# One written-out order for five engines: convolution attention, cosine linear attention and a top-2 expert layer

## The chip, the cores and the metric

The kernel runs on one core of a Trainium2 chip. Its time is the device time of one execution in microseconds (us); the median of several executions is compared. A core has TensorE (PE, matrix products into eight PSUM banks), VectorE (DVE), ScalarE (ACT), GpSimd (POOL) and SyncE (SP). Each works through its own queue in the order in which the program wrote it, and they wait for each other by semaphores.

## The reference

Eight images of 128 channels and 256 positions go through three layers, each with a residual. All numbers are float32.

```python
# layer 0, attention within an image (xf: 128 channels x 256 positions)
q, k, v = wq @ xf + bq, wk @ xf + bk, wv @ xf
sim = softmax(q.T @ k / 8 + (wkm @ xf + bkm), axis=2)
x = x + gamma * (v @ sim.T)
# layer 1, cosine-weighted linear attention over the 8 images: the cumulative sum
# runs over the images, 8 heads of 16; q_, k_ carry sin and cos of the image's angle
n = layernorm(t)
q, k, v = relu(n @ q_w.T + q_b), relu(n @ k_w.T + k_b), n @ v_w.T + v_b
attn[l] = sum(j <= l: (q_[l] . k_[j]) v[j]) / max(sum(j <= l: q_[l] . k_[j]), 1e-6)
t = t + attn @ out_w.T + out_b
# layer 2, two of eight experts for each of 2048 tokens
n = layernorm(t)
w = softmax over the two largest of n @ router_w
t = t + sum(w[e] * ((silu(n @ w1[e]) * (n @ w3[e])) @ w2[e]))
```

## The kernel before

**Front.** Each image i passes some thirty steps on four engines. On TensorE they are `conv_proj_qk`, `conv_proj_v`, `conv_scores`, `conv_turn` (transposes of the probabilities), `conv_out`, then `lin_turn`, `lin_proj_qk`, `lin_proj_v`, `lin_scores`, `lin_scores_turn`, `lin_out_turn`, `lin_out`, then `route_turn`, `route_logits`, `route_rank`. ScalarE evicts PSUM and makes exponentials and, in `route_lean` (L544 to L551), two hyperbolic tangents that give the routing weights. VectorE makes maxima, statistics (`lin_stats`, `lin_moments`), products of q and k with all earlier images (`lin_products`), values, and the routing from `route_top` to `route_slots`. A token's normalisation (`lin_norm` L865, `route_norm` L948) is a VectorE call that subtracts the mean and multiplies by the inverse root. The inverse root is one GpSimd power, `rstd_lin` (L428) and `rstd_ffn` (L435), of a variance to which VectorE has added epsilon (`lin_eps`, `route_eps`).

**Routing to rows.** `route_rank` counts, with products by a triangle of ones, how many tokens before this one chose the same expert; `route_slots` makes of it the row in a buffer `rows_x` in HBM in which each expert has a list of its own. `scatter` (L441), four indirect DMAs for an image on GpSimd's queue, writes the normalised tokens with their weight and destination there.

**Order of the front.** On every engine a loop over steps calls a list of stages, each with a lag: stage s of image i runs in step i + lag. So all engines take the images in lockstep, one step for an image, 20 steps in all. Each kind of PSUM result has one fixed bank, shared by two kinds in places, and `bank_free` makes TensorE wait until the bank's last reader is done.

**Between the stages.** After the last image TensorE counts the tokens of each expert, VectorE makes from the counts, in a dozen small calls, a table of 39 blocks of 128 rows, each with its first row and its expert (L1026 to L1042), and TensorE turns it. Eight DMAs pad the lists of the experts (`pad_lists`, L349), four on SyncE and four on ScalarE. The engines read table entries into registers eight at a time (`table_reader`, L357); the code of SyncE reads the first eight, then waits for the pads and the scatters.

**Expert stage.** For block s SyncE loads 128 rows (ring of 12), TensorE transposes them (`turn_x`), ScalarE evicts the transposed rows, VectorE copies the expert's weights out of a table in SBUF (`weights`), TensorE makes gate and up products (`gate_up`), ScalarE the silu, VectorE the product (`hidden`), TensorE the down product (`down`), VectorE multiplies by the routing weight (`weigh`, L1062), and GpSimd scatters the rows to `rows_y` (L461). The rings are XBT 4, GATE 3, HID 4, WBS 3. Ahead of the first block TensorE runs 16 warm-up matmuls that nobody reads (L778). At the end the two results of each token are loaded in six parts, added to the residual and stored.

Of the kernel before, what the change touches and what calls it, by code (L numbers as in the profile page):

```python
# [7 lines left out]
ALU = mybir.AluOpType  # L8
# [7 lines left out]
P = 128  # L16
B = 8
# [35 lines left out]

# [14 lines left out]
T_ROW, T_EXPERT = range(2)  # L68

# [22 lines left out]
def hybrid_block(nc, x_ch, x_tok, w_conv, w_lin, w_router, w13, w2, vecs, bias_rows, cst_f, cst_tri, cst_dest,  # L92
                 out):
    ctx = ExitStack()
    with ctx:
# [34 lines left out]
        warm = sb("warm", [PROJ + 1, 1])  # L130
# [14 lines left out]
        ve1 = sb("ve1", [P, 2, T])  # L145
        rs1 = sb("rs1", [P, 2, T])
# [17 lines left out]
        ve2 = sb("ve2", [P, 2, T])  # L164
        rs2 = sb("rs2", [P, 2, T])
# [11 lines left out]
        cnt = sb("cnt", [P, E])  # L177
# [23 lines left out]
        y1 = sb("y1", [P, NT, P])  # L201
        y2 = sb("y2", [P, NT, P])
# [16 lines left out]
        ps_aT = bank(BANK_AT)[:, 0:N]
        ps_y = bank(BANK_Y)[:, 0:T * P].rearrange("p (t c) -> p t c", t=T)  # L220

        ps_x2T = bank(BANK_X2T)[:, 0:N]
        ps_log = bank(BANK_LOG)[:, 0:T * E].rearrange("p (t e) -> p t e", t=T)
        ps_rank = bank(BANK_RANK)[:, 0:T * E].rearrange("p (t e) -> p t e", t=T)
        ps_cnt = bank(7)[:, N + 2 * T * E:N + 2 * T * E + E]

        ps_table = bank(7)[0:2, N + 2 * T * E + E:N + 2 * T * E + E + BLOCKS]
        ps_xbT = [bank(n)[:, 0:P] for n in BANKS_XBT]
        ps_yb = [bank(n)[:, 0:P] for n in BANKS_YB]
        ps_warm = bank(5)[:, 0:2 * P]  # L230
        ps_gu = [bank(n) for n in BANKS_GU]
# [3 lines left out]
        ld_x = [sem(f"ld_x{i}") for i in range(B)]  # L235
        ld_vec = sem("ld_vec")
# [26 lines left out]
        ve1_done = sem("ve1_done")  # L263
# [18 lines left out]
        ve2_done = sem("ve2_done")  # L282
# [11 lines left out]
        scattered = sem("scattered")  # L294
# [27 lines left out]
        wb_done = sem("wb_done")  # L322
        yb_done_pe = sem("yb_done_pe")
# [19 lines left out]
        def run_step(step, *stages):  # L343

            for stage, lag, *which in stages:
                if 0 <= step - lag < B:
                    stage(step - lag, *which)
# [22 lines left out]
        def _(sp):  # L370
# [26 lines left out]
            for s in range(BLOCKS):  # L397
# [5 lines left out]
                if s + 1 < BLOCKS:  # L403
                    row = first_row(s + 1)
# [730 lines left out]
```

## Time and profile before

| | |
|---|---|
| median of 3 runs (lowest, highest) | 201.02 us (199.63, 201.24) |
| profiled execution: its time, its span | 201.14 us, 199.3 us |
| TensorE, VectorE, ScalarE, GpSimd busy in the span | 147.9, 126.2, 73.5, 88.2 us |
| mean granted clock of TensorE | 0.858 of full speed |

The span goes from the first to the last instruction that the profiler recorded. A busy share is a mean over stages that are limited by different things, so it is read by stretches. The granted clock has two levels, 2.4 GHz (1.00) and 1.2 GHz (0.50).

### The profile page before, as it was taken

How to read it: one execution, taken by the hardware profiler on the slowest of the kernel's cores; microseconds unless marked ns; L12 is line 12 of the kernel's file. 1: busy time of each engine (PE TensorE's matmuls, PEld its weight loads, DVE VectorE, ACT ScalarE, POOL GpSimd, SP SyncE). 2: the span in 40 equal slices, each digit the busy share in tenths (PEclk: the TensorE clock that was granted, in tenths of full speed). 3: DMA queues.
4: the chain of work that ended last, by engine and by line, in shares of the span. 5: the costliest groups of instructions: out<-in, count | busy, mean ns of one | idle time of the engine just before them, and what ended most of it. 6: DMA issues, size and time to landing. Idle time of an engine off the chain costs nothing.

```text
span 199.3 us, 4128 instructions
## 1 busy us (share of the span) xinstructions
PE 147.9 (74%) x1125; PEld 129.2 (65%) x1125; DVE 126.2 (63%) x464; ACT 73.5 (37%) x222; POOL 88.2 (44%) x94
## 2 busy tenths in 40 slices
PE   0879999999979589684943057999999999992000
PEld 0557788798767457383823045999999999991000
DVE  2526776799989595997365500667767676752263
ACT  2357686667362204221114001444444444440000
POOL 0001111022023718087787750278787878776000
PEclk9999999999999967996555555999999999999555
DMA  5889600000000101011111714223243333110595
GB/s 131 228 265 363 247 3 0 0 3 0 0 5 13 40 0 56 1 43 42 40 57 53 153 48 105 62 79 92 76 100 84 92 92 85 47 53 0 178 251 204
DMA packets 15476, 16.91 MB, mean 85 GB/s; under 512 B 3083, under 2 KB 14032, under 8 KB 15198
## 3 DMA queue, kind: packets, MB, share of 16 engines
q1 hardware_dynamic: 12606, 12.14, 20.8%
q0 software_dynamic: 2272, 4.24, 6.8%
q10 hardware_dynamic: 576, 0.27, 0.8%
q8 instruction: 10, 0.16, 0.4%
q14 instruction: 12, 0.10, 0.2%
HBM read 10.76 MB, written 6.33 MB: 86 GB/s over the span
## 4 chain that ended last, share of the span: by engine, by line
PE 54%; issue 11%; DVE 11%; DMA 8%; POOL 7%; SPq 3%; ACT 3%; POOLq 0%; DVEq 0%; ACTq 0%
PE ps L759 18%; PE ps L768 8%; POOL rows_x L449 4%; PE ps L610 3%; DMA y<-rows_y 3%; PE ps L630 3%; PE ps L750 2%; PE ps L669 2%; PE ps L690 2%; PE ps L595 2%; DVE num L920 2%; DMA XT<-in_x_tok 2%; PE ps L596 2%; PE ps L620 2%; DVE xrow L952 2%
## 5 line engine op out<-in xcount | busy, mean ns | idle before, releaser
L461 POOL DMA_INDIRECT rows_y<-yb,xb x39 | 43.9, 1124 | 21.9 <-DVE yb L1068 21.0
L759 PE MATMUL ps<-xbT,WB 128*128 128x128 f32 x312 | 42.7, 282 | 0.0
L449 POOL DMA_INDIRECT rows_x<-xrow,slot x32 | 32.3, 1008 | 22.8 <-DVE slot L1013 14.2
L759 PEld LDWEIGHTS ps<-xbT,WB 128*128 128x128 f32 x312 | 39.4, 198 | 0.1
L433 POOL TENSOR_TENSOR rs<-ve,CF 128x2 f32<-128x2 f32 x8 | 5.6, 702 | 42.9 <-DVE ve L863 42.9
L1068 DVE TENSOR_SCALAR yb<-ps,xb 128x128 f32<-128x128 f32 x39 | 13.7, 351 | 17.2 <-PE ps L768 17.2
L572 ACT ACTIVATE gate<-ps 128x256 f32<-128x256 f32 x39 | 14.9, 383 | 25.6 <-PE ps L759 25.6
L768 PE MATMUL ps<-W,hid 128*128 x156 | 23.7, 276 | 0.5 <-DVE hid L1051 0.5
L1051 DVE TENSOR_TENSOR hid<-gate,ps 128x256 f32<-128x256 f32 x39 | 16.0, 411 | 11.0 <-ACT gate L572 11.0
L768 PEld LDWEIGHTS ps<-W,hid 128*128 128x128 f32 x156 | 20.5, 192 | 0.7 <-issue 0.7
L566 ACT ACTIVATE xbT<-ps 128x128 f32<-128x128 f32 x39 | 10.8, 277 | 19.3 <-PE ps L750 19.3
L1058 DVE COPY WB<-W 128x512 f32 x39 | 16.3, 421 | 1.5 <-issue 1.5
L750 PE MATMUL ps<-CF,xb 128*128 128x128 f32 x39 | 11.2, 287 | 1.2 <-DMA xb<-rows_x 1.2
L881 DVE TENSOR_TENSOR qk<-kT,qT 128x1024 f32<-128x1024 f32 (+3 forms) x12 | 11.4, 950 | 0.9 <-ACT kT L517 0.9
L920 DVE TENSOR_TENSOR num<-vt,sco 128x1024 f32<-128x1024 f32 (+3 forms) x12 | 11.4, 953 | 0.1
L690 PE MATMUL ps<-CF,num 128*128 128x128 f32 x72 | 11.1, 308 | 0.0
L714 PE MATMUL ps<-WR,x2T 128*128 128x8 f32 x32 | 5.9, 292 | 5.6 <-DVE where L1004 5.6
L714 PEld LDWEIGHTS ps<-WR,x2T 128*128 128x128 f32 x32 | 5.8, 251 | 6.4 <-issue 6.4
L595 PE MATMUL ps<-X,WC 128*65 128x256 f32 x16 | 5.5, 426 | 5.8 <-DMA XT<-in_x_tok 5.8
L690 PEld LDWEIGHTS ps<-CF,num 128*128 128x128 f32 x72 | 9.4, 160 | 0.0
L610 PE MATMUL ps<-ck,cq 65*128 65x256 f32 x32 | 8.7, 396 | 0.1
L630 PE MATMUL ps<-cv,probT 128*128 128x128 f32 x64 | 8.7, 279 | 0.0
(126 smaller groups left out, 281.2 us busy)
## 6 DMA issues: line engine op xcount, KB each, us to landing
xb<-rows_x SPq DMA_DIRECT2D x39, 65.0 KB, 2.0
W<-in_w SPq DMA_DIRECT2D x1, 2048.0 KB, 10.3
y<-rows_y SPq DMA_DIRECT2D x8, 192.0 KB, 4.8
X<-in_x_ch SPq DMA_DIRECT2D x8, 128.0 KB, 2.9
XT<-in_x_tok SPq DMA_DIRECT2D x8, 128.0 KB, 3.4
W<-in_w SPq DMA_DIRECT2D x1, 1024.0 KB, 12.4
out_tok<-y SPq DMA_DIRECT2D x4, 192.0 KB, 3.6
rows_y<-yb,xb POOLq DMA_INDIRECT x39, 2.4
```

Source lines behind the costliest of these rows:

```text
L449: pool.indirect_dma_start(rows_x, bass.IndirectOffsetOnAxis(ap=slot[:, g:g + 1], axis=0), xrow[:, i * T + t, c, :], None, bounds_check=DUM ...
L461: pool.indirect_dma_start(rows_y, bass.IndirectOffsetOnAxis(ap=xb[:, n, DEST_COL:ROW].bitcast(I32), axis=0), yb[:, n, :], None, bounds_che ...
L572: act.activation(gate[:, s % GATE, :], ps_gu[s % 3][:, 0:F], ACT.Silu).then_inc(gate_done, 1)
L610: last = pe.matmul(ps_sim[:, t, :], cq[:, b, t * P:(t + 1) * P], ck[:, b, :], start=True, stop=True)
L630: last = pe.matmul(ps_co[:, t, :], probT[:, b, k, t * P:(t + 1) * P], cv[:, b, k, :], start=(k == 0), stop=(k == T - 1))
L690: last = pe.matmul(ps_aT[:, t * P:(t + 1) * P], num[:, i % 2, j, t * P:(t + 1) * P], ident, start=(j == 0 and t == 0), stop=(j == i), is_t ...
L750: pe.transpose(ps_xbT[s % 2], xb[:, s % RING, 0:P], ident).then_inc(xbT_done, 1)
L759: last = pe.matmul(ps_gu[s % 3][:, k * P:(k + 1) * P], WB[:, s % WBS, k * P:(k + 1) * P], xbT[:, s % XBT, :], start=True, stop=True)
L768: last = pe.matmul(ps_yb[s % 2], hid[:, s % HID, k * P:(k + 1) * P], W2[:, bass.ds(e * (FK * P) + k * P, P)], start=(k == 0), stop=(k == F ...
L920: dv.tensor_tensor(num[:, b, first:end, :].rearrange("p j (g d) -> p (j g) d", d=D), vt[:, first:end, :].rearrange("p j (g d) -> p (j g) d ...
L1051: dv.tensor_tensor(hid[:, s % HID, :], gate[:, s % GATE, :], ps_gu[s % 3][:, F:2 * F], ALU.mult)\
L1058: dv.tensor_copy(WB[:, s % WBS, :], W13[:, bass.ds(experts[s] * (2 * F), 2 * F)]).then_inc(wb_done, 1)
```

## The change

1. All five queues are written out call by call instead of in lockstep steps. TensorE, VectorE and ScalarE take the calls of different images in one mixed order, and PSUM banks are given call by call (`BANK_CQK = (1, 3, 5, 0, ...)`): any result may stand in any of the eight banks, in one rotation with the others.
2. Both normalisations become ScalarE activations (scale and bias from SBUF columns). The epsilon, a negated mean and the product of it with the inverse root move to GpSimd, two of them with a wait on GpSimd's own results. The weighting of the expert results moves to ScalarE as well.
3. Scatters are written out one by one on GpSimd, with inverse roots of later images among them.
4. Loads: the weights of the first layer, constants, triangles, destinations and router weights go out on ScalarE's queue; the two layouts of an image have a semaphore each, and TensorE waits for the channel layout alone.
5. The table code can make several tables; there is one, of 39 blocks. It stands ahead of the last `route_slots` on VectorE. All eight pads are issued by SyncE, which reads its first table entries after the waits.
6. The table load for the silu (`silu_set`) stands on ScalarE after the last exponential, ahead of six of the eight `route_lean` calls. The warm-up matmuls are gone.
7. Rings: XBT 6, GATE 4, HID 5, WBS 5. In the expert stage TensorE transposes the rows of six blocks in a batch. The arrays of the final sums reuse the inputs' SBUF.

```diff
-XBT, GATE, HID, WBS = 4, 3, 4, 3
-BANKS_XBT, BANKS_GU, BANKS_YB = (0, 1), (3, 4, 6), (2, 5)
+XBT, GATE, HID, WBS = 6, 4, 5, 5
+TABLES = ((8, 39, 0),)
...
-            sp.wait_ge(table_done, 1)
-            first_row = table_reader(sp, T_ROW, DUMMY)
-            row = first_row(0)
-            sp.wait_ge(pads_stored, 16 * (E + 1))
-            sp.wait_ge(scattered, 16 * NT * TOP_K)
...
+                sp.wait_ge(table_done, k + 1)
...
+                    sp.wait_ge(scattered[n], 16 * images * T * TOP_K)
...
+                    sp.wait_ge(pads_stored, 16 * (E + 1))
+                for s in range(first, first + blocks):
+                    load_rows(s)
...
             def rstd_ffn(i):
-                pool.wait_ge(ve2_done, i + 1)
+
+                b = i % 2
+                pool.wait_ge(mv2_done, 2 * (i + 1))
                 if i >= 2:
                     pool.wait_ge(xrow_done, 2 * (i - 1))
-                pool.tensor_tensor(rs2[:, i % 2, :], ve2[:, i % 2, :], CF[:, C_HALF:C_HALF + T], ALU.pow).then_inc(rs2_done, 1)
...
+                pool.tensor_scalar(nm2[:, b, :], mv2[:, b, :, 0], -1.0, None, ALU.mult)
+                link(pool.tensor_scalar(ve2[:, b, :], mv2[:, b, :, 1], LN_EPS, None, ALU.add))
+                link(pool.tensor_tensor(rs2[:, b, :], ve2[:, b, :], CF[:, C_HALF:C_HALF + T], ALU.pow))
+                pool.tensor_tensor(nb2[:, b, :], nm2[:, b, :], rs2[:, b, :], ALU.mult).then_inc(rs2_done, 1)
...
-            for step in range(STEPS):
-                run_step(step, (scatter, 9, 0), (scatter, 9, 1), (rstd_lin, 2), (rstd_ffn, 6))
...
+            rstd_lin(0); rstd_lin(1); rstd_lin(2); rstd_lin(3); rstd_ffn(0); rstd_lin(4); rstd_ffn(1)
+            scatter(0, 0); scatter(0, 1); scatter(0, 2); scatter(0, 3); rstd_lin(5); rstd_ffn(2); scatter(1, 0)
+            scatter(1, 1); scatter(1, 2); rstd_lin(6); scatter(1, 3); rstd_ffn(3); scatter(2, 0); scatter(2, 1)
+            scatter(2, 2); rstd_lin(7); scatter(2, 3); rstd_ffn(4); scatter(3, 0); scatter(3, 1); scatter(3, 2)
+            scatter(3, 3); rstd_ffn(5); scatter(4, 0); scatter(4, 1); scatter(4, 2); scatter(4, 3); rstd_ffn(6)
+            scatter(5, 0); scatter(5, 1); scatter(5, 2); scatter(5, 3); rstd_ffn(7); scatter(6, 0)
...
+            def route_norm(i):
+                b = i % 2
+                act.wait_ge(rs2_done, i + 1)
+                for t in range(T):
+                    act.activation(xrow[:, i * T + t, :, 0:P], t2[:, i * T + t, :].unsqueeze(1).broadcast_to([P, TOP_K, P]),
+                                   ACT.Identity, bias=nb2[:, b, t:t + 1], scale=rs2[:, b, t:t + 1]).then_inc(xrow_done, 1)
...
+            lin_v(3); conv_qk(7); conv_pT(6); conv_v(6); route_lean(1); lin_sums(4); lin_norm(5); conv_exp(7)
+            silu_set(); route_norm(2); lin_xT(5); lin_aT(3); lin_v(4); route_xT(2); conv_pT(7); lin_qk(5)
...
-            for step in range(STEPS):
-                run_step(step, (lin_scores_turn, 5), (lin_proj_qk, 4), (lin_proj_v, 5), (route_rank, 9), (conv_proj_v, 1), (lin_out_turn, 6),
-                         (conv_turn, 2), (conv_scores, 1), (route_logits, 8), (lin_out, 6), (lin_turn, 3), (conv_out, 2),
-                         (lin_scores, 4, 0), (conv_proj_qk, 0), (lin_scores, 4, 1), (route_turn, 7))
...
+            conv_proj_v(0); conv_proj_qk(0); conv_scores(0); conv_proj_qk(1); conv_proj_v(1); conv_proj_qk(2)
+            conv_turn(0); conv_scores(1); conv_proj_qk(3); conv_out(0); conv_scores(2); conv_turn(1)
+            conv_proj_v(2); conv_scores(3); conv_out(1); conv_proj_qk(4); conv_turn(2); conv_proj_v(3)
+            conv_turn(3); lin_turn(0); conv_proj_qk(5); conv_out(2); lin_proj_qk(0); lin_turn(1); lin_proj_v(0)
...
+            conv_proj_v(5); route_turn(0); lin_out(1); lin_out_turn(2); route_logits(0); lin_turn(4)
+            lin_scores(3, 0); conv_out(5); conv_scores(6); route_rank(0); lin_proj_qk(4); lin_out(2)
...
-            for _ in range(WARM_MATMULS):
-                pe.matmul(ps_warm, TRI[:, 0:P], TRI[:, :], start=True, stop=True)
...
+            down(16); gate_up(18); down(17); gate_up(19); turn_x(20); down(18); turn_x(21); turn_x(22)
+            turn_x(23); turn_x(24); turn_x(25); gate_up(20); down(19); gate_up(21); gate_up(22); down(20)
...
+            route_where(6); route_slots(6); route_top(7); route_index(7); route_gap(7); route_mask(7)
+            route_seen(7); route_weights(7); route_where(7); table_rows(0); route_slots(7); table_copy(0)
```

## Rows read from the trace of the kernel before

**Rows 1.** The page's busy tenths, 40 slices of 5 us.

```profile
PE   0879999999979589684943057999999999992000
DVE  2526776799989595997365500667767676752263
ACT  2357686667362204221114001444444444440000
POOL 0001111022023718087787750278787878776000
```

**Rows 2.** Windows: us, busy (instructions) of PE, PEld, DVE, ACT, POOL; clock, DMA, GB/s.

```profile
70.00:71.00 1.00, 0.28 (x3) 0.30 (x3) 1.00 (x3) 0.00 (x0) 0.00 (x0) 0.96 0.00 0
77.00:78.00 1.00, 1.00 (x5) 0.82 (x5) 0.76 (x4) 0.00 (x0) 0.73 (x1) 0.63 0.28 83
125.00:126.00 1.00, 1.00 (x9) 1.00 (x8) 0.71 (x2) 0.00 (x0) 0.00 (x0) 0.74 0.37 75
130.00:150.00 20.00, 20.00 (x182) 20.00 (x181) 13.98 (x42) 9.19 (x28) 15.73 (x15) 1.00 0.33 86
```

**Rows 3.** The chain that ended last: start, us, what; the last scatter.

```profile
116.98 2.28 DMA rows_x<-xrow,slot
```

**Rows 4.** Timeline of GpSimd, 60 to 120 us: start, us, what, [idle before].

```profile
62.78 1.19 POOL L449 DMA_INDIRECT rows_x<-xrow,slot  x1 [4.46 <-DVE slot L1013]
...
107.91 0.97 POOL L449 DMA_INDIRECT rows_x<-xrow,slot  x1 [0.30 <-issue]
109.18 0.97 POOL L449 DMA_INDIRECT rows_x<-xrow,slot  x1 [0.30 <-issue]
```

**Rows 5.** Timeline of all engines, from the count to the last block.

```profile
108.90 0.17 DVE L1026 COPY cnt<-ps 128x8 f32<-128x8 f32 x1 [0.35 <-PE ps L742]
...
109.98 1.93 SPq L355 DMA_DIRECT2D rows_x<-pad  x4
...
111.36 0.14 DVE L1042 TENSOR_SCALAR steer<-exp_f 39x1 f32<-39x1 f32 x1
...
113.45 1.12 DVE L1058 COPY WB<-W 128x512 f32 x3 [1.45 <-issue]
...
121.49 1.01 PE L750 MATMUL ps<-CF,xb 128*128 128x128 f32 x2 [1.18 <-DMA xb<-rows_x]
...
180.48 0.71 PE L768 MATMUL ps<-W,hid 128*128 x4 [0.52 <-DVE hid L1051]
```

**Rows 6.** The same chain at 21 us: TensorE at full clock.

```profile
21.51 0.45 PE ps L602 x4
...
22.39 0.87 PE ps L610 x4
```

**Rows 7.** Waits: who waited for whom: us in total, times, longest.

```profile
PE ps L595 <- DMA XT<-in_x_tok: 5.8, 1, 5.8
```

**Rows 8.** DMA issues: count, size, median us to landing.

```profile
xb<-rows_x SPq DMA_DIRECT2D x39, 65.0 KB, 2.0
...
X<-in_x_ch SPq DMA_DIRECT2D x8, 128.0 KB, 2.9
...
WC<-in_w_conv SPq DMA_DIRECT2D x1, 129.0 KB, 2.5
```

**Rows 9.** Groups by line: count, busy us, mean ns of one, idle before.

```profile
L439 POOL TENSOR_TENSOR rs<-ve,CF 128x2 f32<-128x2 f32 x8 | 5.9, 743 | 0.0
L425 POOL COPY xrow<-DEST 128x32 int32<-128x32 int32 x1 | 0.2, 240 | 7.3 <-DMA DEST<-in_cst_dest 7.3
L423 POOL MEMSET pad<- 128x1 int32 x1 | 0.1, 102 | 0.0
L488 ACT ACTIVATE cv<-ps,VEC 128x256 f32<-128x256 f32 x8 | 3.8, 473 | 1.1 <-PE ps L602 1.1
L536 ACT ACTIVATE attT<-ps 128x256 f32<-128x256 f32 x8 | 3.1, 384 | 7.7 <-PE ps L690 7.7
L566 ACT ACTIVATE xbT<-ps 128x128 f32<-128x128 f32 x39 | 10.8, 277 | 19.3 <-PE ps L750 19.3
L558 ACT ACT_TABLE_LOAD x1 | 1.3, 1283 | 0.0
```

More of the change, by code:

```diff
@@ L68 @@
 T_ROW, T_EXPERT = range(2)
+NO_EXPERT = 1 << 14
 def constants():
@@ L293, in hybrid_block @@
         slot_done = sem("slot_done")
-        scattered = sem("scattered")
+        scattered = [sem(f"scattered{k}") for k in range(len(TABLES))]
         cnt_done = sem("cnt_done")
@@ L322, in hybrid_block @@
         wb_done = sem("wb_done")
+        wb_loaded = [sem(f"wb_loaded{n}") for n in range(WBS)]
         yb_done_pe = sem("yb_done_pe")
@@ L341, in pieces, with table_of @@
             return sum(len(halves(i)) for i in range(n))
[L343 to L347, printed above, removed]
-        def pad_lists(eng, experts):
-            eng.wait_ge(pad_row_done, 1)
-            held = [eng.alloc_register(f"pad_row{e}") for e in experts]
-            eng.reg_load(held, pad_row[0:1, experts[0]:experts[-1] + 1])
-            for reg in held:
-                row = eng.snap(reg, min_val=0, max_val=DUMMY - P)
-                eng.dma_start(rows_x[bass.ds(row, P), :], pad[:, :]).then_inc(pads_stored, 16)
+        def table_of(s):
+            return [k for k, (_, _, first) in enumerate(TABLES) if first <= s][-1]
         def table_reader(eng, line, most):
             sets = [[eng.alloc_register(f"line{line}_{half}_{n}") for n in range(READ)] for half in range(2)]
+            turn = [1]
             def read(s):
-                held = sets[s // READ % 2]
-                if s % READ == 0:
-                    m = min(READ, BLOCKS - s)
-                    eng.reg_load(held[0:m], table[line:line + 1, s:s + m])
-                return eng.snap(held[s % READ], min_val=0, max_val=most)
+                _, blocks, first = TABLES[table_of(s)]
+                n = (s - first) % READ
+                if n == 0:
+                    turn[0] = 1 - turn[0]
+                    m = min(READ, first + blocks - s)
+                    eng.reg_load(sets[turn[0]][0:m], table[line:line + 1, s:s + m])
+                return eng.snap(sets[turn[0]][n], min_val=0, max_val=most)
             return read
@@ L459, in _, with result @@
+            def result(s):
                 n = s % RING
@@ L1070, in _ @@
-            dv.wait_ge(ld_w13, 32)
-            dv.wait_ge(table_done, 1)
-            expert = table_reader(dv, T_EXPERT, E - 1)
-            experts = [expert(0)]
-            for s in range(-3, BLOCKS + 1):
-                if s + 3 < BLOCKS:
-                    weights(s + 3)
-                if s >= 1:
-                    weigh(s - 1)
-                if 0 <= s + 1 < BLOCKS:
-                    hidden(s + 1)
+                dv.tensor_copy(WB[:, s % WBS, :], W13[:, bass.ds(e * (2 * F), 2 * F)]).then_inc(wb_done, 1)
```

665 lines of the change are left out of this document (406 added, 259 removed).

## The prediction, made before the changed kernel ran

> **What bounds the kernel now.** I read the busy tenths first, then the chain that ended last, the timeline around the change of stage, and the groups for prices. The tenths [rows 1] show three stages. Up to the 10th slice (50 us) TensorE fills nearly every slice after the first. From there to the 24th no engine is full for long: TensorE falls from 9 to 0, VectorE stands at 9 and then between 6 and 3, while GpSimd climbs to 7 and 8. From the 26th slice TensorE is full again until the outputs are gathered. So a front with slack is followed by a mixture-of-experts (MoE) stage without any. In the window 130 to 150 us [rows 2] TensorE is busy all 20.0 us with 182 matmuls; a block has 13 (8, 4 and 1 by line), so 14 blocks pass at 1.43 us each. VectorE, ScalarE and GpSimd are busy 14.0, 9.2 and 15.7 us there: no reordering makes that stage shorter than 39 x 1.43 = 55.7 us.
>
> What ends the front is GpSimd. The last row scatter starts at 116.98 us and its data land 2.28 us later [rows 3]. Before it the scatters run back to back: one starts 1.27 us after the other with only "issue" between them [rows 4]. The first of 32 starts at 62.78, having waited 4.46 us for a slot number [rows 4]. So the front is set by when routing of image 0 is ready and by how tightly 32 scatters and the inverse roots, all on GpSimd's queue, follow. The span divides at rows thus: 116.98 to the last scatter; 4.51 to the first row transpose at 121.49 [rows 5]; 59.70 of blocks to the end of the last down projection (180.48 + 0.71 = 181.19 [rows 5]); 18.11 to the end at 199.30.
>
> **First scatter.** The chain gives TensorE's prices at full clock [rows 6]: 0.45 us for four passes of 128 columns (a four-tile transpose is the same), 0.87 for four passes of 256. In TensorE's new order there stand ahead of the first ranking: 7 query/key projections of 0.87 (6.1), 6 value projections (2.7), 7 score pairs (6.1), 6 four-tile transposes (2.7), 6 outputs of eight passes (5.4), and of the linear attention 5 turns, 4 and 3 projections, scores, turns and outputs of up to four images (some 11, priced by the same passes): 34 us. The first matmul waits until 5.80 for the second layout of image 0 [rows 7], which it doesn't read; afterwards it waits for the channel layout and the weights alone, and the weights go out on ScalarE's queue. A channel layout lands 2.9 us after its issue and the weights 2.5 [rows 8], both issued by about 0.8: 3.7 us. With 3 us for the exchanges with ScalarE and VectorE in the first images and 1.8 for ranking to slots, the first scatter starts at 42.5 us instead of 62.78.
>
> **The GpSimd queue after it.** 31 more starts at 1.28 are 39.7 us. Nine inverse-root calls stand among them in the new order (images 5 to 7 of the first normalisation, 2 to 7 of the second). Such a call was one power of 0.743 us [rows 9]; now it is four instructions with two waits on GpSimd's own results. The trace of before has no such small arithmetic on GpSimd. From below, a 128x1 memset takes 0.102; from above, the power itself is a two-operand instruction of 0.743; nearest in kind is a 128x32 copy of 0.240 [rows 9]. I take 0.2 each with one of the three overlapped, and 0.1 for each own wait: 1.4 us, bounds 0.8 and 3.1. Nine are 12.6 us. What waits behind them on the queue: a scatter ready to go, and behind the scatters the roots, so normalisation 6 waits for the scatters of image 4, and 7 for those of image 5. I allow 6 us in which the queue has nothing to do: about 2 for image 2's slots, 1.5 for image 5's moments, 2.5 at the end, because VectorE now makes the block table before the slots of image 7. From the count's copy at 108.90 to the second column at 111.36 that took 2.6 us [rows 5]; in before the slots went first. Last scatter: 42.5 + 39.7 + 12.6 + 6.0 = 100.8 us, 16.2 earlier.
>
> **VectorE and ScalarE.** 32 normalisation calls and the 39 weightings leave VectorE, with 16 additions of epsilon. ScalarE pays more per call: a pointer operand is worth 473 - 384 = 89 ns [rows 9], so weighting costs 0.277 [rows 9] + 0.089 = 0.37, and a normalisation with two pointers 0.46 (128 wide) or 0.56 (256 wide): 16 us in the front. It has the room: 5 to 8 tenths up to the 10th slice, mostly 4 or less after it [rows 1]. In the MoE stage ScalarE goes from 0.66 us a block (9.2 over 14 [rows 2]) to 1.03, under 1.43. I cost it at nothing there: TensorE covers it, and per-block cost would show only above 1.43.
>
> **Between the stages.** SyncE used to read its first registers before it waited for the scatters; now it reads them after. VectorE shows what a read costs: 1.45 us idle with "issue" ahead of its first weight copy [rows 5]. Bounds 0.2 and 1.45; I take 1.3. All eight list pads now go out on SyncE, one after the other, instead of four each on two queues; four took 1.93 to issue [rows 5]. Eight issues at 0.48 end some 4 us after the count and land near the last scatter, which covers them; uncovered they would cost 1 us. Stage: 4.51 + 1.3 = 5.8.
>
> **Blocks.** The 16 warm-up matmuls go. The clock row shows 1.2 GHz up to the middle of 125 to 126 us, some 4.0 us after the first transpose; earlier, with nothing ahead of it, it fell at the end of 70 to 71 and rose again 6.7 us later [rows 2]. At half speed 6.7 us lose 3.35 of work against 2.0: +1.4, bounds 0 and 2. Deeper rings and batches of six transposes move no TensorE work; the sixth transpose of a batch needs a buffer whose result left 7.3 us of TensorE work earlier, and the way round (weighting 0.5, scatter and landing near 2.3 [rows 3], reload 2.0 [rows 8], issue 0.5 each) takes some 6. The end is 0.7 shorter, since the last results queue less. So 59.7 + 1.4 and 18.1 - 0.7.
>
> **Sum.** 100.8 + 5.8 + 61.1 + 17.4 = 185.1 us of span. The profiled execution took 201.14 at a span of 199.3, so 1.84 lie around it: 186.9, say **187 us**. That execution is within 0.1% of the median of 201.02.
>
> **The Trainium skill against the change.** The page "GPSIMD Engine Reference", opening, calls GpSimd the wrong choice for ordinary elementwise arithmetic, VectorE being about twice as fast; this change moves the epsilon and the negated mean there. The trace has only the 0.240 us copy to weigh it with, and neither settles calls on two columns; by twice VectorE's price the call would be about 1.5, and the sum 188. The page "ScalarE: Activation LUTs", section "Table sets: the hidden batching unit", asks to finish one set before going to the next, 2.66 us a switch with the drain. The trace has a load of 1.283 us [rows 9] for the gate's function, after the last hyperbolic tangent; now it stands ahead of twelve of these.
>
> **Rivals.**
> 1. GpSimd nearly packed: the small calls cost their lower bound, image 0 is ready at 40. 40 + 39.7 + 9 x 0.83 + 3 = 90.2, 10.6 less: 176 us. For it: at the end GpSimd's scatters were packed in before too [rows 4]. Against: each image's routing needs a full turn through all engines.
> 2. Slower: each small GpSimd call costs as much as the power. 4 x 0.743 + 0.1 = 3.1 us a call, 1.7 x 9 = 15.3 more on the queue that ends the front: 202 us. It decides from 2.95 us a call (1.4 + 14 / 9). For it: the only two-operand row is 0.743. Against: copy and memset, a third and a seventh of that.
> 3. ScalarE becomes the bound: the hyperbolic tangents have to reload their table (two more loads, one in front of the first gate, 2.6 us), and its written order blocks on inverse roots that wait behind scatters, 2.5 us more: 192 us.
> 4. The order doesn't fill the front: image 0 is ready only at 48, and from first to last scatter it takes as long as before (116.98 - 62.78 = 54.2) plus nine longer calls, 6 us: 108, 7.3 later than my sum: 194 us.
>
> **Chances.** The forecast 0.52, with its own range of 182 to 191; rival 1 0.15, rival 2 0.07, rival 3 0.14, rival 4 0.12. The range 177 to 198 leaves out half of rival 1, rival 2 and the upper end of rival 4, under 0.2; it takes in the bounds of register read and clock, and all of the small calls' but their upper end. A measurement of this kernel tells 1% from nothing (its runs lie 0.8% apart). Faster by over 1%, below 199.0: 0.90; within: 0.04; slower: 0.06.
>
> **What would show it.** Right: the first scatter near 42 and the last near 101 us; TensorE at 8 tenths or more up to some 60 us; inverse-root groups of four instructions at about 1.4 us; blocks again at 1.43; SyncE idle over a microsecond between landing and first load; the low clock for some microseconds more in the first blocks. Wrong: small GpSimd instructions of 0.5 us or more, a third table load, TensorE waiting at every sixth transpose, or scatters that wait for slots for more than 6 us in all.

## The result, and the profile after

The changed kernel takes 204.22 us (median of 4 runs, 203.01 to 205.92), 1.0224 times the kernel before, with a 95% interval of 1.0151 to 1.0298. It is slower, by 1.5 to 3%; forecast was 187.0, 177 to 198. The ratios here and below are estimated from the faster executions alone and are not quotients of the medians, which here give 204.22 / 201.13 = 1.0154. The profiled execution took 203.01 us at a span of 201.1.

The busy tenths of the page, 40 slices of 5.0 us, answer to [rows 1]:

```profile
PE   1899999999959783995453104999999999995000
DVE  2066466969716586479141620354554545531163
ACT  3277997787376643432313001456566565653000
POOL 0002331545868588787777450157667676767000
```

TensorE is full from the 3rd slice to the 10th and VectorE has more room, as forecast. But GpSimd, which climbs earlier, stands at 5 to 8 from the 11th slice to the 22nd: it starts sooner and ends no sooner. The timeline of GpSimd, 40 to 130 us (start, us, what, [idle before]), answers to [rows 4]:

```profile
47.81 2.15 POOL L502 DMA_INDIRECT rows_x<-xrow,slot  x1 [2.12 <-DVE slot L1133]
50.27 0.98 POOL L502 DMA_INDIRECT rows_x<-xrow,slot  x1 [0.31 <-issue]
51.55 2.00 POOL L502 DMA_INDIRECT rows_x<-xrow,slot  x1 [0.30 <-issue]
53.85 0.97 POOL L502 DMA_INDIRECT rows_x<-xrow,slot  x1 [0.30 <-issue]
...
70.61 1.70 POOL L502 DMA_INDIRECT rows_x<-xrow,slot  x1 [1.83 <-DVE slot L1133]
72.61 0.98 POOL L502 DMA_INDIRECT rows_x<-xrow,slot  x1 [0.30 <-issue]
...
80.16 1.81 POOL L489 TENSOR_TENSOR rs<-ve,CF 128x2 f32<-128x2 f32 x1
...
84.32 1.86 POOL L502 DMA_INDIRECT rows_x<-xrow,slot  x1 [0.30 <-issue]
...
87.76 1.64 POOL L502 DMA_INDIRECT rows_x<-xrow,slot  x1 [0.30 <-issue]
89.47 0.23 POOL L487 TENSOR_SCALAR nm<-mv 128x2 f32<-128x2 f32 x1
89.76 0.22 POOL L488 TENSOR_SCALAR ve<-mv 128x2 f32<-128x2 f32 x1
90.06 0.72 POOL L489 TENSOR_TENSOR rs<-ve,CF 128x2 f32<-128x2 f32 x1
90.86 0.20 POOL L490 TENSOR_TENSOR nb<-nm,rs 128x2 f32<-128x2 f32 x1
91.75 1.09 POOL L502 DMA_INDIRECT rows_x<-xrow,slot  x1 [0.70 <-issue]
...
114.26 0.96 POOL L502 DMA_INDIRECT rows_x<-xrow,slot  x1 [2.42 <-DVE slot L1133]
...
118.26 0.97 POOL L502 DMA_INDIRECT rows_x<-xrow,slot  x1 [0.30 <-issue]
```

The first scatter starts 15 us earlier than before and the last 1.3 us later [rows 3, 4]: 31 starts take 70.45 us instead of 54.2. What follows the last scatter is much as forecast. Timelines of SyncE and TensorE, between the stages and at the last block, then the window 130 to 150 (columns as in [rows 2]):

```profile
121.34 4.12 SPq L416 DMA_DIRECT2D xb<-rows_x  x8
...
123.42 0.45 PE L868 MATMUL ps<-CF,xb 128*128 128x128 f32 x1 [9.77 <-DMA xb<-rows_x]
...
183.63 0.71 PE L894 MATMUL ps<-W,hid 128*128 x4 [0.67 <-DVE hid L1193]
...
130.00:150.00 20.00, 20.00 (x182) 20.00 (x181) 10.56 (x28) 12.47 (x42) 13.64 (x14) 1.00 0.29 80
```

Against the sum: first scatter 47.81 (forecast 42.5), from it to the last 70.45 (58.3), to the first row transpose 5.16 (5.8), blocks to 183.63 + 0.71 = 184.34, so 60.92 (61.1), tail 201.1 - 184.34 = 16.76 (17.4). Late by 5.3 and 12.15, early by 1.4: 16.0 us of span. The profiled run lies 1.2 us below the median, which is the rest. Again 182 matmuls pass in 20 us: the bound of the expert stage (TensorE's 1.43 us a block) has not moved.

**Where the 70.45 us are.** Clean scatters: 31 x 1.28 = 39.7. Root calls: the scatter before the call at 89.47 ends at 89.40 and the next starts at 91.75; of these 2.35 us 0.30 would be there anyway, so a call takes 2.05 us of the queue, and nine take 18.5. Waits for slots: 1.83 us at 70.61, of which 0.69 belong to the call ahead, and 2.42 at 114.26, of which 0.30 are usual, so 3.3. Stretched instructions: 9 scatters of 1.05 to 2.15 us instead of 0.97, one at 1.15 and four root instructions lie 9 us above their usual length. Together 70.5. The 54.2 us of before divide as 39.7 + six roots at 0.64 (3.8) + two waits of 4.6 (9.2) + 1.3 of stretch = 54.0, from rows of before that were not shown yet (GpSimd's timeline):

```profile
74.09 1.10 POOL L449 DMA_INDIRECT rows_x<-xrow,slot  x1 [4.88 <-DVE slot L1013]
...
84.65 1.10 POOL L449 DMA_INDIRECT rows_x<-xrow,slot  x1 [4.88 <-DVE slot L1013]
...
101.81 0.74 POOL L439 TENSOR_TENSOR rs<-ve,CF 128x2 f32<-128x2 f32 x1
102.73 1.04 POOL L449 DMA_INDIRECT rows_x<-xrow,slot  x1 [0.18 <-issue]
```

A power alone: the scatter before it ended at 101.79, the next starts at 102.73; 0.94 - 0.30 = 0.64.

**What stretches a scatter.** VectorE's timeline of the changed kernel beside the rows above: `qk` and `num` (L1015, L1052) multiply two operands that both lie in SBUF.

```profile
47.65 1.22 DVE L1015 TENSOR_TENSOR qk<-kT,qT 128x1024 f32<-128x1024 f32 x1
...
51.48 1.23 DVE L1052 TENSOR_TENSOR num<-vt,sco 128x1024 f32<-128x1024 f32 x1
...
73.15 0.95 DVE L1015 TENSOR_TENSOR qk<-kT,qT 128x768 f32<-128x768 f32 x1
...
80.16 1.22 DVE L1052 TENSOR_TENSOR num<-vt,sco 128x1024 f32<-128x1024 f32 x1
...
84.12 1.23 DVE L1015 TENSOR_TENSOR qk<-kT,qT 128x1024 f32<-128x1024 f32 x1 [2.74 <-ACT kT L596]
...
87.35 1.21 DVE L1015 TENSOR_TENSOR qk<-kT,qT 128x1024 f32<-128x1024 f32 x1
```

The scatter at 51.55 meets `num` with 51.48 + 1.23 - 51.55 = 1.16 us to go and takes 2.00; that at 84.32 meets `qk` with 1.03 to go: 1.86; at 87.76 with 0.80 to go: 1.64. Each takes 0.84 plus what the product still has to run, or 0.97 if that is more. In all sixteen traces 63 scatters that follow another scatter begin at least 0.06 us into such a product, and all but one of them keep to this within 0.03 us. A scatter that follows arithmetic or a wait pays up to 0.26 more (the first, with 1.06 to go, takes 2.15). The scatter at 72.61, in whose course a product begins, takes 0.98, and one that begins with the product, within 0.03 us, mostly isn't held either (at 66.01: 1.10). The expert stage gives the other half of the comparison; VectorE and GpSimd of the changed kernel, then of the kernel before:

```profile
145.06 0.41 DVE L1193 TENSOR_TENSOR hid<-gate,ps 128x256 f32<-128x256 f32 x1
...
145.19 0.97 POOL L510 DMA_INDIRECT rows_y<-yb,xb  x1 [0.30 <-issue]
```

```profile
139.68 0.42 DVE L1058 COPY WB<-W 128x512 f32 x1
...
139.80 1.14 POOL L461 DMA_INDIRECT rows_y<-yb,xb  x1 [0.30 <-DVE yb L1068]
```

`hid` has one operand in PSUM: all 11 scatters that start under it, with up to 0.35 us to go, take 0.97. The copy of weights from SBUF to SBUF, with 0.30 to go, gives 1.14 = 0.84 + 0.30, as for the 35 scatters of before that start under it (mean 1.15). So operands decide, not VectorE being busy; e3 and e4 below show it for one product in one place. The Trainium skill has this in "GPSIMD Engine Reference", section "1. Specifications": GpSimd's SBUF interfaces are shared with VectorE, with contention when a VectorE instruction has two SBUF inputs or runs in its two-port mode. The rows of `qk`, `num` and `hid` agree; whether the copy, which has one input, runs in the two-port mode no row shows. The prediction left this out.

### The profile page after: what moved, and what is told of

Read it like the earlier page. It is cut to its first block, busy times and chain, and to the rows that moved or that the text cites. A ratio compares the mean times of both kernels' runs of the same rounds, so it can differ in the third digit from the quotient of the medians.

```text
span 201.1 us, 4097 instructions
## 1 busy us (share of the span) xinstructions
PE 146.7 (73%) x1109; PEld 129.3 (64%) x1109; DVE 101.8 (51%) x377; ACT 97.0 (48%) x294; POOL 102.5 (51%) x142
## 4 chain that ended last, share of the span: by engine, by line
PE 55%; POOL 17%; issue 11%; DMA 7%; DVE 4%; SPq 2%; ACT 2%; POOLq 0%; ACTq 0%; DVEq 0%
PE ps L879 17%; POOL rows_x L502 10%; PE ps L894 8%; PE ps L723 4%; PE ps L804 3%; PE ps L743 3%; PE ps L868 2%; POOL rows_y L510 2%; DMA X<-rows_y 2%; PE ps L707 2%; PE ps L708 2%; PE ps L715 2%; PE ps L759 2%; PE ps L782 2%; DMA WC<-in_w_conv 2%
## 5 line engine op out<-in xcount | busy, mean ns | idle before, releaser
L510 POOL DMA_INDIRECT rows_y<-yb,xb x39 | 37.9, 972 | 28.9 <-ACT yb L661 23.1
L502 POOL DMA_INDIRECT rows_x<-xrow,slot x32 | 38.2, 1194 | 17.6 <-issue 11.3
L1193 DVE TENSOR_TENSOR hid<-gate,ps 128x256 f32<-128x256 f32 x39 | 16.2, 415 | 5.1 <-PE ps L894 3.7
L661 ACT ACTIVATE yb<-ps,xb 128x128 f32<-128x128 f32 x39 | 14.3, 367 | 3.4 <-PE ps L894 1.6
L647 ACT ACTIVATE xbT<-ps 128x128 f32<-128x128 f32 x39 | 8.5, 280 | 13.6 <-PE ps L868 13.6
L868 PE MATMUL ps<-CF,xb 128*128 128x128 f32 x39 | 7.6, 300 | 10.0 <-DMA xb<-rows_x 10.0
L1015 DVE TENSOR_TENSOR qk<-kT,qT 128x1024 f32<-128x1024 f32 (+3 forms) x12 | 11.5, 955 | 5.3 <-ACT kT L596 5.3
L621 ACT ACTIVATE xrow<-t,nb,rs 128x256 f32<-128x256 f32 x16 | 8.7, 593 | 10.1 <-POOL nb L490 10.1
L1052 DVE TENSOR_TENSOR num<-vt,sco 128x1024 f32<-128x1024 f32 (+3 forms) x12 | 11.4, 953 | 1.8 <-ACT vt L609 1.6
L476 POOL TENSOR_SCALAR nm<-mv 128x2 f32<-128x2 f32 x8 | 2.8, 344 | 18.5 <-DVE mv L1007 18.3
L868 PEld LDWEIGHTS ps<-CF,xb 128*128 128x128 f32 x39 | 5.4, 156 | 10.4 <-issue 10.4
L581 ACT ACTIVATE xn<-t,nb,rs 128x128 f32<-128x128 f32 x16 | 7.0, 486 | 8.1 <-POOL nb L479 8.0
L979 DVE TENSOR_REDUCE nmax<-ps 128x2 f32<-128x512 f32 x8 | 5.5, 687 | 10.3 <-PE ps L723 10.2
```

Of the source, the lines that this page charges most:

```text
L502: pool.indirect_dma_start(rows_x, bass.IndirectOffsetOnAxis(ap=slot[:, g:g + 1], axis=0), xrow[:, i * T + t, c, :], None, bounds_check=DUM ...
L510: pool.indirect_dma_start(rows_y, bass.IndirectOffsetOnAxis(ap=xb[:, n, DEST_COL:ROW].bitcast(I32), axis=0), yb[:, n, :], None, bounds_che ...
L661: act.activation(yb[:, n, :], bank(BANK_YB[s])[:, 0:P], ACT.Copy, scale=xb[:, n, W_COL:W_COL + 1]).then_inc(yb_done, 1)
L868: pe.transpose(bank(BANK_XBT[s])[:, 0:P], xb[:, s % RING, 0:P], ident).then_inc(xbT_done, 1)
L1015: dv.tensor_tensor(qk[:, i % 2, first:end, :], kT[:, first:end, :], qT[:, i % 2, :].unsqueeze(1).broadcast_to([P, end - first, N]), ALU.mult)\
L1193: dv.tensor_tensor(hid[:, s % HID, :], gate[:, s % GATE, :], bank(BANK_GU[s])[:, F:2 * F], ALU.mult)\
```

## The experiments

Ratios are to the kernel before, measured on the same chip; the experiments ran on several chips, on which it had medians of 199.99 to 200.72 us, so a difference in us between two of them is good to about 1 us. Theory Q is: GpSimd's queue ends the front, and each microsecond in it counts. Theory O: the order, in which roots stand behind scatters, holds the images.

**e1: small calls off GpSimd.** VectorE adds epsilon and negates, GpSimd makes the power alone, ScalarE the shift `nb`.

```diff
-                pool.tensor_scalar(nm1[:, b, :], mv1[:, b, :, 0], -1.0, None, ALU.mult)
-                link(pool.tensor_scalar(ve1[:, b, :], mv1[:, b, :, 1], LN_EPS, None, ALU.add))
-                link(pool.tensor_tensor(rs1[:, b, :], ve1[:, b, :], CF[:, C_HALF:C_HALF + T], ALU.pow))
-                pool.tensor_tensor(nb1[:, b, :], nm1[:, b, :], rs1[:, b, :], ALU.mult).then_inc(rs1_done, 1)
+                pool.tensor_tensor(rs1[:, b, :], ve1[:, b, :], CF[:, C_HALF:C_HALF + T], ALU.pow).then_inc(rs1_done, 1)
...
```

> The changed kernel, but GpSimd computes only the power: VectorE adds epsilon and negates the mean right after the moments, ScalarE multiplies the negated mean by the root (two 0.2 us calls and an own wait). Theory Q (GpSimd's queue ends the front; a root call of four instructions costs it 2.05 us from the end of one scatter to the next, a single power 0.64): nine calls among the scatters save 9 x 1.4 = 12.7 us, of which some 8 to 12 arrive, 192 to 196 us; last scatter at 106 to 110 us instead of 118. Rival O (the mixed order itself delays the images and GpSimd only waits for them): 203 to 205 us, GpSimd idle longer between scatters.

Measured: 198.69 us, 0.9912 [0.9864, 0.996]; first scatter 49.23, last 114.71. Between the two theories: the last scatter comes 3.5 us earlier, not the 9 x (2.05 - 0.64) = 12.7 that nine calls would give. When a call shrinks, part of it becomes waiting: among its scatters GpSimd now waits some 13 us for moments and slots, against 3.3.

**e2: the kernel before, with three small calls and two own waits beside each power** (their results unread).

```diff
-                pool.tensor_tensor(rs1[:, i % 2, :], ve1[:, i % 2, :], CF[:, C_HALF:C_HALF + T], ALU.pow).then_inc(rs1_done, 1)
+                pool.tensor_scalar(xa[:, 2 * i + 0, :], CF[:, C_HALF:C_HALF + T], -1.0, None, ALU.mult)
+                link(pool.tensor_scalar(xe[:, 2 * i + 0, :], CF[:, C_HALF:C_HALF + T], LN_EPS, None, ALU.add))
+                link(pool.tensor_tensor(rs1[:, i % 2, :], ve1[:, i % 2, :], CF[:, C_HALF:C_HALF + T], ALU.pow))
+                pool.tensor_tensor(xp[:, 2 * i + 0, :], xa[:, 2 * i + 0, :], rs1[:, i % 2, :], ALU.mult).then_inc(rs1_done, 1)
...
```

> The kernel before, in its lockstep order, with three small calls beside each power on GpSimd, as many as in the changed kernel and with the same two own waits, their results unused (nothing is left out). Theory Q: three to six of the calls stand among back-to-back scatters, each 1.4 us longer: 205 to 209 us, last scatter at 121 to 125. Rival O: within 1 us of 201.

Measured: 208.98 us (four runs, 207.02 to 210.75) beside 200.67; the profiled one took 207.78. First scatter 65.56 instead of 62.78, last 124.02 instead of 116.98. GpSimd's timeline:

```profile
107.87 0.22 POOL L454 TENSOR_SCALAR xe<-CF 128x2 f32<-128x2 f32 x1
108.17 0.72 POOL L455 TENSOR_TENSOR rs<-ve,CF 128x2 f32<-128x2 f32 x1
108.97 0.20 POOL L456 TENSOR_TENSOR xp<-xa,rs 128x2 f32<-128x2 f32 x1
109.85 1.09 POOL L466 DMA_INDIRECT rows_x<-xrow,slot  x1 [0.69 <-issue]
```

In the lockstep order too the four instructions cost, some 7 us for sixteen calls: 2.8 ahead of the first scatter and 4.3 behind it, where six of them stand. The next scatter starts 0.69 us after the last of them instead of 0.18. Theory Q holds for the calls' price.

**e3 and e4: one more 128x256 product per block in the expert stage,** on the changed kernel; in e3 both operands in SBUF, in e4 one in PSUM.

```diff
+                link(dv.tensor_tensor(hid[:, s % HID, :], gate[:, s % GATE, :], W13[:, 0:F], ALU.mult))
                 dv.tensor_tensor(hid[:, s % HID, :]
```

> The changed kernel with one extra VectorE product of 128x256 in each of the 39 blocks, both inputs in SBUF (overwritten at once by the right product, after an own wait). Theory C (GpSimd's work stands still while VectorE runs a two-input call with both inputs in SBUF, which stretched scatters of the front from 0.97 to 2.15 us): the block scatters, 0.972 us in the changed kernel, get a longer mean, 1.1 us or more, some of 1.3 to 1.5. Rival T (scatters stretch by their own data or the DMA queue): 0.97 as before. The time within 2 us of 204, VectorE having room.

> The same extra product in the same place with one input in PSUM. Theory C: the block scatters stay at 0.97 to 1.0 us. A theory by which any more VectorE work stretches them: as long as in the SBUF run.

Measured: 208.48 and 207.49 us, one run each, more than the 2 us from 204 that were expected; why stays open. Scatters took 0.995 and 0.986 us on average, because most begin when no extra product runs. The few that begin under one settle it. VectorE and GpSimd of e3, then of e4 (the upper line of each is the extra product):

```profile
184.69 0.42 DVE L1193 TENSOR_TENSOR hid<-gate,W 128x256 f32<-128x256 f32 x1 [0.96 <-PE ps L894]
...
184.81 1.16 POOL L510 DMA_INDIRECT rows_y<-yb,xb  x1 [0.31 <-issue]
```

```profile
183.71 0.42 DVE L1193 TENSOR_TENSOR hid<-gate,ps 128x256 f32<-128x256 f32 x1 [0.96 <-PE ps L894]
...
183.82 0.97 POOL L510 DMA_INDIRECT rows_y<-yb,xb  x1 [0.30 <-issue]
```

Both scatters begin with some 0.31 us of the extra product to go. With both operands in SBUF the scatter takes 0.84 + 0.31, with one in PSUM its usual 0.97. Three more of e3, with 0.18 to 0.19 to go, take 1.02 to 1.04; two more of e4, with 0.15 and 0.19 to go, take 0.97. So theory C's stretch is there and rival T's 0.97 isn't, though with four such scatters of 39 the mean doesn't reach the 1.1 that was expected.

**e5: only GpSimd's order changed,** roots ahead of the scatters of two images earlier.

```diff
-            scatter(0, 0); scatter(0, 1); scatter(0, 2); scatter(0, 3); rstd_lin(5); rstd_ffn(2); scatter(1, 0)
-            scatter(1, 1); scatter(1, 2); rstd_lin(6); scatter(1, 3); rstd_ffn(3); scatter(2, 0); scatter(2, 1)
+            rstd_lin(5); rstd_ffn(2); scatter(0, 0); scatter(0, 1); scatter(0, 2); scatter(0, 3);
+            rstd_lin(6); scatter(1, 0); scatter(1, 1); rstd_ffn(3); scatter(1, 2); scatter(1, 3);
+            rstd_lin(7); scatter(2, 0); scatter(2, 1); rstd_ffn(4); scatter(2, 2); scatter(2, 3);
...
```

> The changed kernel with nothing but GpSimd's written order altered: each inverse root stands one to four calls earlier, ahead of scatters whose data nobody waits for until the end (root 5 of the first normalisation and 2 of the second ahead of the scatters of image 0, and so on). Theory H (roots that wait behind scatters hold up the images, because every other queue stands in order behind the normalisation): the first-layer output of image 3 leaves its last addition near 55 us instead of 63, last scatter at 108 to 113 instead of 118, 195 to 200 us. Rival Q (only the sum of work on GpSimd's queue counts, which is the same): 203 to 205.

Measured: 200.55 us, 1.0016 [0.9956, 1.0077], between the two theories. The order is worth something by itself, some 4 us; why not more, e8 shows.

**e6: the slots of image 7 ahead of the table, and SyncE reads a block's register before it waits.**

```diff
-route_where(7); table_rows(0); route_slots(7); table_copy(0)
+route_where(7); route_slots(7); table_rows(0); table_copy(0)
...
```

> The changed kernel with the slots of image 7 ahead of the block table on VectorE, and SyncE reading its first table entries ahead of its waits, as in the kernel before. Theory: the 2.42 us in which GpSimd waits for the last slots go, and of the 0.80 us between the last landing and the first row load 0.6 goes: 200.5 to 202 us. Rival (the table, now later, or the pads take the place of the scatters as what SyncE waits for): 203 to 205.

Measured: 201.28 us, 1.011 [0.9954, 1.0265]; last scatter 116.21 instead of 118.26. The time is as expected, but its interval overlaps the changed kernel's, so the 2 us rest on the trace: the table that VectorE makes first is the 2.42 us in front of the scatter at 114.26.

**e7: the products cut into pieces of 128x256,** same arithmetic.

```diff
-                dv.tensor_tensor(qk[:, i % 2, first:end, :], kT[:, first:end, :],
-                                 qT[:, i % 2, :].unsqueeze(1).broadcast_to([P, end - first, N]), ALU.mult)\
-                  .then_inc(qk_done, 1)
+                for j in range(first, end):
+                    last = dv.tensor_tensor(qk[:, i % 2, j:j + 1, :], kT[:, j:j + 1, :], qT[:, i % 2, :].unsqueeze(1), ALU.mult)
+                last.then_inc(qk_done, 1)
...
```

> The changed kernel with VectorE's long products (queries with keys, weights with values, up to 128x1024, 1.22 us, both inputs in SBUF) cut into one call of 128x256 for each image, 48 calls more. Theory C (a GpSimd instruction that begins while such a product runs waits for its end): row scatters fall from a mean of 1.194 us to 1.02 to 1.10, none over 1.5, and if GpSimd's queue counts, 199 to 203 us in spite of some 3 us more on VectorE. Rival T (the stretch has nothing to do with VectorE): mean still 1.15 to 1.20 with some of 1.8 or more, 204 to 207 us.

Measured: 198.67 us, 0.9941 [0.9894, 0.9988], although the products themselves take longer. Groups by line:

```profile
L502 POOL DMA_INDIRECT rows_x<-xrow,slot x32 | 34.0, 1062 | 16.9 <-issue 11.2 <-DVE slot L1134 5.6
...
L1016 DVE TENSOR_TENSOR qk<-kT,qT 128x256 f32<-128x256 f32 x36 | 13.1, 418 | 4.1 <-ACT kT L596 4.1
```

The scatters fall from 1.194 to 1.062 us, the last starts at 114.46. The stretch is VectorE's doing, as e3 beside e4 has it too.

**e12: the same cut on the kernel before.**

> The kernel before with VectorE's long products cut into pieces of 128x256. Theory C and the lockstep order: its scatters were hardly stretched (mean 1.008 us), so nothing is won and 3 us of VectorE are added in a stretch where VectorE was at 8 to 9 tenths: 201 to 204 us. If the cut itself makes VectorE's or TensorE's work faster (so that the 5.5 us which it gave the changed kernel have nothing to do with GpSimd): 196 to 199.

Measured: 201.67 us, 1.011 [1.0063, 1.0158]. In the lockstep order of the kernel before such a product was running when one of 32 scatters began (at 88.59, 1.22 us), so cutting them only costs. The stretch is a price of the new overlap.

**e8: e1, the order of e5, and e6 together.**

> The changed kernel with three edits together: small calls off GpSimd (as in the first run), roots ahead of scatters, slots and register read early. If the three delays add up, 5.5 (measured) + 5 to 8 + 3 leave 187 to 191 us, faster than the kernel before; if they are the same wait seen three times, 195 to 199.

Measured: 197.09 us, 0.9874 [0.9742, 1.0005]; not additive. GpSimd's timeline:

```profile
64.95 1.23 POOL L492 TENSOR_TENSOR rs<-ve,CF 128x2 f32<-128x2 f32 x1 [4.28 <-DVE nm L1097]
...
73.67 0.72 POOL L492 TENSOR_TENSOR rs<-ve,CF 128x2 f32<-128x2 f32 x1 [1.45 <-DVE nm L1097]
...
85.21 0.72 POOL L492 TENSOR_TENSOR rs<-ve,CF 128x2 f32<-128x2 f32 x1 [4.98 <-DVE nm L1097]
```

Three roots that wait for their moments hold the queue for 10.7 us, with scatters of earlier images ready behind them; a fourth, at 96.36, holds it for 3.3.

**e9: e8 with those scatters ahead of such roots.**

```diff
-            rstd_lin(6); scatter(1, 0); scatter(1, 1); rstd_ffn(3); scatter(1, 2); scatter(1, 3);
-            rstd_lin(7); scatter(2, 0); scatter(2, 1); rstd_ffn(4); scatter(2, 2); scatter(2, 3);
+            rstd_lin(6); scatter(1, 0); scatter(1, 1); scatter(1, 2); scatter(1, 3); rstd_ffn(3);
+            scatter(2, 0); scatter(2, 1); rstd_lin(7); scatter(2, 2); scatter(2, 3); rstd_ffn(4);
...
```

> The kernel of all three edits (197.1 us) with GpSimd's order written after its trace: the roots of images 3 to 7 stand where their moments come, and the scatters that are ready fill the 14 us of holes in which GpSimd waited for roots. Theory Q+H (GpSimd's queue and its order set the end, the ten scatters that ran back to back after the last slots at 102.5 us were backlog): last scatter near 108 to 110 instead of 114, 191 to 194 us. Rival I (the images' own way through the other engines ends the front): 196 to 198.

Measured: 192.91 us, 0.9673 [0.9605, 0.9742], better than both kernels. Its first and last scatter:

```profile
52.53 1.19 POOL L504 DMA_INDIRECT rows_x<-xrow,slot  x1 [0.33 <-issue]
...
109.44 0.97 POOL L504 DMA_INDIRECT rows_x<-xrow,slot  x1 [0.30 <-issue]
```

From first to last 56.9 us; the last ten stand back to back.

**e10 and e11: e9 with cut products; e9 with 16 warm-up matmuls ahead of the first block.**

> The same with VectorE's products cut into 128x256 pieces. With few stretched scatters left, theory C gives at most 2 us, and 48 more calls cost VectorE some 3: between 1 us less and 3 us more than the run without the cut.

> The same as the first of these with the 16 warm-up matmuls before the first row transpose again, into a free bank, after the pads have landed. The kernel before, with them, ran its blocks at 1.2 GHz for 4.0 us after the first transpose, the changed one for some 5.4: 0.5 to 1.5 us less than without. If the clock rises as late with them: no change.

Measured: 193.18 us, 0.9661 [0.9584, 0.9738], and 192.43 us, 0.9654 [0.9576, 0.9732]. Neither differs from e9. In e9 scatters wait for slots at 67.58 and 87.63 us, and a stretch ahead of a wait would cost nothing; that may explain e10, but wasn't tried by itself. The warm-up does lift the clock in the first blocks; TensorE had been idle for 8.0 us in e9, and runs its 16 matmuls from 111.26 in e11. Windows of e9, then of e11:

```profile
115.00:120.00 5.00, 5.00 (x31) 5.00 (x31) 1.51 (x4) 1.95 (x8) 0.00 (x0) 0.64 0.46 106
```

```profile
115.00:120.00 5.00, 4.17 (x35) 3.93 (x36) 1.51 (x4) 2.21 (x10) 0.24 (x1) 1.00 0.44 106
```

Four more matmuls pass in these 5 us, but the first transpose came 0.5 us later (114.28 instead of 113.75).

**e13: e9's order with the changed kernel's four-instruction roots.**

```diff
-                pool.tensor_tensor(rs1[:, b, :], ve1[:, b, :], CF[:, C_HALF:C_HALF + T], ALU.pow).then_inc(rs1_done, 1)
+                pool.tensor_scalar(nm1[:, b, :], mv1[:, b, :, 0], -1.0, None, ALU.mult)
+                link(pool.tensor_scalar(ve1[:, b, :], mv1[:, b, :, 1], LN_EPS, None, ALU.add))
+                link(pool.tensor_tensor(rs1[:, b, :], ve1[:, b, :], CF[:, C_HALF:C_HALF + T], ALU.pow))
+                pool.tensor_tensor(nb1[:, b, :], nm1[:, b, :], rs1[:, b, :], ALU.mult).then_inc(rs1_done, 1)
...
```

> The changed kernel with the GpSimd order in which ready scatters fill the holes, the slots of image 7 ahead of the table and the early register read, but with the roots still four GpSimd instructions each, as changed. Theory Q (a root call costs 2.05 us of the queue, against some 1.0 for the power alone): nine calls cost about 9 us where the queue is full and part of it where holes hide them, so 197 to 200 us, the last scatter near 113. Theory O (it was the order of roots and scatters alone, the four instructions fit into holes): 192 to 194.5 us, as the same order with the power alone (192.9).

Measured: 198.31 us, 0.9935 [0.9889, 0.9982]; last scatter 113.28. Theory Q: the small calls cost some 5 us (0.9935 against 0.9673) even in an order with room for roots. And order with e6 alone brings the changed kernel from 1.0224 to 0.9935.

**e14: e9's order with both normalisations back on VectorE.**

```diff
-                    act.activation(xn[:, b, t, :], t1[:, i, t, :], ACT.Identity, bias=nb1[:, b, t:t + 1], scale=rs1[:, b, t:t + 1])
...
+                    dv.tensor_scalar(xn[:, i % 2, t, :], t1[:, i, t, :], mv1[:, i % 2, t, 0:1],
+                                     rs1[:, i % 2, t:t + 1], ALU.subtract, ALU.mult).then_inc(xn_done, 1)
...
```

> The same order, slots and register read, with both normalisations back on VectorE as in the kernel before (VectorE adds epsilon, GpSimd makes only the power, VectorE subtracts and multiplies in one call); weighting stays on ScalarE. Theory M (the move to ScalarE was worth something: VectorE regains about 10 us of work in a front where it is at 4 to 6 tenths, and its written order now waits for roots): 195 to 200 us. Theory N (the move was worth nothing or harmful, since it needs a negated mean and a shift, and ScalarE waits for roots in its written order): 189 to 193 us. With the same order and ScalarE normalisations it is 192.9.

Measured: 199.8 us, 0.9947 [0.9893, 1.0001]; first scatter 54.28, last 115.85. In this order ScalarE's normalisations are worth 5 to 7 us (by the ratios 0.9947 against 0.9673, by the medians 199.8 against 192.91), so that part of the change helps. It holds for the one place in VectorE's order that was tried, three calls after the moments; VectorE then waits there for roots, as ScalarE does otherwise (groups of e14, with the idle time before them):

```profile
L1008 DVE TENSOR_SCALAR xrow<-t,mv,rs 128x256 f32<-128x256 f32 x16 | 5.9, 413 | 4.6 <-POOL rs L491 4.5
L1002 DVE TENSOR_SCALAR xn<-t,mv,rs 128x128 f32<-128x128 f32 x16 | 4.9, 348 | 3.6 <-POOL rs L483 3.6
```

## Why the prediction was wrong

**The step that failed** is "The GpSimd queue after it", with the sum that ends "Last scatter: 42.5 + 39.7 + 12.6 + 6.0 = 100.8 us, 16.2 earlier". It came at 118.26: 5.3 us from the first scatter, and 12.15 from the queue behind it. That queue's account above against the sum's terms gives 9.0 of stretch for which there was no term, 18.5 for 12.6 of root calls, and 3.3 for 6.0 of waits. Three of its assumptions fell.

- *A scatter every 1.28 us.* That price was read at the end of the front, where no such product ran beside the scatters [rows 4]. Put beside the products, nine of them were held, and some roots: 9 us, for which the sum had no term. e7 takes 5.5 us off the whole by cutting the products; the old order paid 1.3 us of it, and e12 shows that cutting gains nothing there.
- *A root call at 1.4 us.* The instructions were priced nearly right (0.23 + 0.22 + 0.72 + 0.20 = 1.37, own waits 0.07 to 0.08). Missed were that none overlaps another (1.59 from start to end) and that the next scatter then starts 0.69 us later where no instruction of the call was held, while it follows a lone power after 0.18. 2.05 instead of 1.4, nine times: 5.9 us. e2 confirms it on the kernel before, e13 beside e9.
- *6 us in which the queue has nothing to do.* In the queue's own account it was 3.3, so this was not short. But the written order also cost images on the other engines, which waited for roots standing behind scatters; ScalarE stood idle for 18 us ahead of its normalisations, all but 1.9 of it for roots that stood behind scatters (groups, answering to the idle columns of [rows 9]):

```profile
L621 ACT ACTIVATE xrow<-t,nb,rs 128x256 f32<-128x256 f32 x16 | 8.7, 593 | 10.1 <-POOL nb L490 10.1
...
L581 ACT ACTIVATE xn<-t,nb,rs 128x128 f32<-128x128 f32 x16 | 7.0, 486 | 8.1 <-POOL nb L479 8.0
```

  With the queue as full as it was, late images did not show as holes in it; once it was shortened they did (e1, e8), and only the order with ready scatters ahead of waiting roots gave the time back (e9 against e8: 0.9874 to 0.9673).

**First scatter**: 47.81 against 42.5. TensorE's start (4.15 for 3.7) and the way from ranking to scatter (2.4 for 1.8) were nearly right; TensorE was busy without a gap from 10 to 46 us, and the calls ahead of the first ranking at 45.39 took 41.2 us where 34 + 3 were counted. TensorE was busy for 40.3 of them, so the mechanism stood, but the count of work was 6 us short, and of the 3 us for exchanges hardly one came.

**Right**: the stage between (5.16 for 5.8, so 0.65 more than before where 1.3 was added), blocks at 1.43 us, 60.92 of blocks with a clock that stayed low longer (0.61 of full speed from 125 to 130 us, 0.95 before), 16.76 of tail, ScalarE's prices (486, 593 and 367 ns for 0.46, 0.56 and 0.37), and that ScalarE has the room. Its table was loaded twice in all, at 1283 ns each, the second before twelve of the tangents: none reloaded it, and rival 3's first half fell. Its second half, ScalarE waiting for roots behind scatters, came true as a wait, the 18 us above, but ScalarE didn't become the bound; what the wait cost by itself no run shows (e5, which moves the roots alone, gains some 4 us).

**The rivals.** Rival 4 had the first scatter (48) and too short a queue: 60 us. Rival 2 had the sign and the queue, but not the price: a small call takes 0.22, not 0.743; that its 202 us came nearest is luck. The mechanism that decided, VectorE's products holding GpSimd together with a queue that was already full, stood in no rival. Its condition could be seen in the change: `qk` and `num` were to run in the very stretch into which the scatters moved.

How much each cause is worth by itself stays open, since they hide each other: off the changed kernel small calls give 5.5 us, cut products 5.5, order 4, e6 some 3 (not clear of its interval); calls, order and e6 together (e9) give 11.3, and in that order cutting gives nothing more.

## What to carry to other kernels

When work is moved into another stretch, its price moves too: look at what the neighbouring engine runs there, and for GpSimd at VectorE's products of two SBUF operands and its large copies within SBUF. An instruction on a full queue costs its gaps as well, so read the price from the end of the instruction before to the start of the one behind, with and without it. In a queue written out by hand, set ready work ahead of work that waits, and remember that a shorter queue first turns into waiting.

## What was not expected of the hardware

- A GpSimd instruction that begins while VectorE runs a product of two SBUF operands, or a 128x512 copy from SBUF to SBUF, ends as if most of it could run only when that is over: 0.84 us plus the rest for a scatter of 0.97, 1.81 for a power of 0.72 that began with a product of 1.22. Begun before the product, it isn't held (0.98). Under a product with one PSUM operand it isn't either (0.97, 11 times, and in e4).
- After the four instructions with two own waits the next indirect DMA starts 0.69 us later and takes 1.09 us (0.17 and 0.55 later where an instruction of the call had been held); after a lone power 0.18 and 1.04. Whether the own waits or the short last instruction (0.20 us against 0.74) make the gap, no run tells apart.
